# A constant row of a graph network: from a product on TensorE to an addition on VectorE

## The chip, the cores and the metric

One core of a Trainium2 chip runs the whole program in one launch. It has five engines with a queue of instructions each: PE (matrix products into PSUM), DVE (elementwise work, scans), ACT (activations and copies), POOL (here: indirect gathers) and SP (here: plain transfers). ACT issues transfers too. Engines wait for one another by semaphores. The metric is the device time of the program in microseconds (us).

## The reference

Two layers of a graph network on 100000 nodes and 50000 edges. In the first, rows of 32 edge values are summed, averaged and maximised over the edges of each source node, and a small network of two layers turns the 97 values of a node into 64:

```
h = concatenate([seg_sum, seg_max, seg_mean, u[batch]], axis=1)
h = relu(h @ W1 + b1)
x = x + (h @ W2 + b2)
h = jnp.maximum(_layernorm(x), 0.0)
agg = segment_sum(h[src], dst)
x = x + relu(agg @ W.T + b)
```

A node without edges still gets relu(u W1 + b1) @ W2 + b2, a constant row. The kernel adds that row to every node, and to the nodes with edges only the difference to it; so "layer two minus the constant" has to be formed for each of them.

## The kernel before

The edges are sorted by node on the chip (up to about 190 us of the profile). Then a **first pass** works through them in 98 steps (BLOCKS) of 512 edges, in 4 tiles (BT) of 128 rows; a **second pass** does the same for the second layer with other instructions, which the change doesn't touch. The order of each engine's queue is written out by hand: the engines run loops of their own over n, and in step n an engine takes different blocks for different jobs.

Step n of the first pass, engine by engine:

- POOL: four gathers of edge values for block n (L576), with waits for DVE's scans, dense additions and one-hots of earlier blocks.
- DVE: the two scans of block n (L1127, L1129), from PSUM p_g and the rows c_rows into feats; the dense addition of block n-7 (L1159); the scaling of gathered values of block n+2 (L1115); the one-hots of block n-5 (L1140).
- PE: the transposes of block n+1 (L1378) into p_g; the expansion of block n-6 (L1408 and L1403, one-hots times records, into p_t or p_u); layer two of block n-1 (function layer2); layer one of block n (L1383, from feats into p_z). An f32 product shows as two MATMUL records.
- ACT: the activation of block n-1 (L719, from p_z into hid); in every second step three loads of rows (L715); the record of block n-1 (L725 and L726) and its store (L731); two of the eight windows of block n-3 (L709, after registers with their starts are loaded, L701).
- SP: six windows of block n-3 (L406), and the dense rows in and out.

Layer two writes one PSUM tile, p_m[0], of 4 x 64 columns. It begins with one bf16 product of three ones rows with nc3, the negated constant split into three bf16 parts (L1389), which fills all 256 columns; the four products with W2 (L1391) add to it. They wait for the activation (hid_ok) and for the previous block's sums to be copied (copied). A record is 66 values for each edge: the 64 sums, the node's number as a key, and a pad. ACT writes it: `record` copies the key, then the sums, and `store_rec` sends it to memory; a ring of four holds the records. nc3 is made once, during the sort, by constant_c and three_parts on DVE beside a turn of the sort.

Of the kernel before, what the change touches and what calls it, by code (L numbers as in the profile page):

```python
# [9 lines left out]
BF16 = mybir.dt.bfloat16  # L10
F16 = mybir.dt.float16
ALU = mybir.AluOpType
# [56 lines left out]
def valid(n):  # L69

    return 0 <= n < BLOCKS


def build(nc, x, src, dst, edge_attr, u, W1, b1, W2, b2, W, b, out):
# [5 lines left out]
    with ExitStack() as ctx:  # L80
        def sb(name, shape, dt=F32):
            return ctx.enter_context(nc.sbuf_tensor(name, shape, dt))
# [4 lines left out]
        def sem(name):  # L87
            return ctx.enter_context(nc.semaphore(name))
# [6 lines left out]

        ident = sb("ident", [P, P])
        one = sb("one", [P, P])
        one_b = sb("one_b", [P, P], BF16)
        pos_i = sb("pos_i", [P, COLS], I32)
        pos_f = sb("pos_f", [P, COLS])  # L100
        next_pos = sb("next_pos", [P, COLS])
# [28 lines left out]
        r0 = sb("r0", [P, P])  # L130
        c_neg = sb("c_neg", [P, D])
        added_rows = sb("added_rows", [P, D])
        nc3 = sb("nc3", [P, BT, D], BF16)
        part_b = [sb(f"part_b{q}", [P, D], BF16) for q in range(2)]
        part_f = [sb(f"part_f{q}", [P, D]) for q in range(3)]
        c_bc = sb("c_bc", [P, D])
        relub = sb("relub", [P, D])

# [125 lines left out]
        rows_in = two("rows_in")  # L264
        scaled, turned, scanned, feats_ok = sem("scaled"), sem("turned"), sem("scanned"), sem("feats_ok")
        z_ok, hid_ok, m_ok = sem("z_ok"), sem("hid_ok"), sem("m_ok")
        copied = sem("records_copied")
        rec_out = several("rec_out", RRING)
        win_in = several("win_in", WRING)
        hot_ok, expanded, added = sem("hot_ok"), sem("expanded"), sem("added")  # L270
# [36 lines left out]
        def delta(k):  # L307
            side, n = divmod(k, BLOCKS)
            return p_d[side][n % len(p_d[side])][:, 0:BT * D].rearrange("p (t d) -> p t d", d=D)
# [201 lines left out]
        def _(pool):  # L511
# [3 lines left out]
            def link(ins):  # L515
                step[0] += 1
                ins.then_inc(s_pool, 1)
                pool.wait_ge(s_pool, step[0])
# [18 lines left out]
            link(g.tensor_scalar(span_f[:, :], prow_i[:, 0:SPAN], 0.5, None, ALU.add))  # L537
            link(g.memset(eps_t[:, :], EPS))
            link(g.memset(one[:, :], 1.0))
            link(g.memset(one_b[:, :], 1.0))  # L540
            link(g.memset(wrong[:, :], 0.0))
            link(g.memset(pad_rec[:, :], -1.0))
            link(g.memset(gagg[D:D + 1, :], 1.0))
# [101 lines left out]
        def _(act):  # L645
# [76 lines left out]
            def record(side, n):  # L722
                k = BLOCKS * side + n
                act.wait_ge(m_ok, k + 1)
                s.copy(rec[k % RRING][:, :, KEY], rn[side][:, BT * n:BT * (n + 1)])  # L725
                s.copy(rec[k % RRING][:, :, 0:D], delta(k)).then_inc(copied, 1)  # L726

            def store_rec(side, n):
                k = BLOCKS * side + n
                act.wait_ge(copied, k + 1)  # L730
                s.dma_start(rec_rows(side, n), rec[k % RRING][:, :, :].rearrange("p t r -> p (t r)")).then_inc(rec_out[k % RRING], 16)  # L731

# [63 lines left out]
        def _(dve):  # L796
# [44 lines left out]
                link(v.tensor_scalar(dummy_f[:, :], srcs_i[:, :], float(BLOCKS * STEP), None, ALU.add))  # L841
                link(v.tensor_scalar(next_pos[:, :], pos_f[:, :], 1.0, None, ALU.add))

            def three_parts(row, at):

                link(v.tensor_copy(part_b[0][:, :], row[:, :]))
                link(v.tensor_tensor(part_f[0][:, :], row[:, :], part_b[0][:, :], ALU.subtract))
                link(v.tensor_copy(part_b[1][:, :], part_f[0][:, :]))
                link(v.tensor_tensor(part_f[1][:, :], part_f[0][:, :], part_b[1][:, :], ALU.subtract))
                link(v.tensor_scalar(part_f[1][:, :], part_f[1][:, :], ident[:, at + 2:at + 3], None, ALU.mult))  # L850
                link(v.scalar_tensor_tensor(part_f[2][:, :], part_b[1][:, :], ident[:, at + 1:at + 2], part_f[1][:, :], ALU.mult, ALU.add))
                link(v.scalar_tensor_tensor(part_f[1][:, :], part_b[0][:, :], ident[:, at + 0:at + 1], part_f[2][:, :], ALU.mult, ALU.add))

            def constant_c():

                three_parts(c_neg, 0)
                link(v.tensor_copy(nc3[:, :, :], part_f[1][:, :].unsqueeze(1).to_broadcast([P, BT, D])))

            def constant_rows():

                link(v.tensor_scalar(part_f[1][:, :], c_bc[:, :], ident[:, CONST[0]:CONST[0] + 1], None, ALU.mult))
                link(v.scalar_tensor_tensor(added_rows[:, :], b_bc[:, :], ident[:, CONST[1]:CONST[1] + 1], part_f[1][:, :], ALU.mult, ALU.add))
                v.tensor_copy(rowmax[:, :], eps_t[:, :]).then_inc(s_wts, 1)

            def bounds(first_node_i):
# [36 lines left out]
            def beside_turn(t):  # L902

                if t == 0:
                    dve.wait_ge(s_const, 1)
                    dve.wait_ge(s_dstl, 96)
                    bounds(dn_i[:, 0:1])
                elif t == 1:
                    dve.wait_ge(s_dcast, 1)
                    link(v.tensor_tensor(ends[:, 1:COLS], dn_f[:, 1:COLS], dn_f[:, 0:COLS - 1], ALU.is_lt))  # L910
                elif t == 3:
                    link(v.reduce_sum(wrong[:, 2:3], ends[:, 1:COLS], AX.X))
                elif t == 6:
                    full = E // COLS
                    v.tensor_tensor(wrong[0:full, 3:4], pair[0:full, 1:2], pair[0:full, 0:1], ALU.is_lt)
                elif t == 4:
                    halves_first()
                elif t == 5:
                    row_of_empty()
                elif t == 7:  # L920
                    weights_turned()
                elif t == 8:
                    constant_c()
                elif t == 9:
                    constant_rows()
                elif t == 11:
                    positions()
# [216 lines left out]
            def add_dense(side, m):  # L1144
# [16 lines left out]
                    ins = v.scalar_tensor_tensor(dout[pair_ % ORING][:, b_, :], to[:, :], 0.0, din[pair_ % 2][:, b_, :], ALU.max, ALU.add)  # L1161
                ins.then_inc(added, 1)

            dve.wait_ge(s_cast, 2)
            dve.wait_ge(s_near, 1)
            dve.wait_ge(s_col, 1)
# [2 lines left out]
            for n in range(BLOCKS + SRC_ADD):  # L1169
                if valid(n):  # L1170
                    scans(n)
                if valid(n - SRC_ADD):
                    add_dense(0, n - SRC_ADD)
                if valid(n + 2):
                    scale_attr(n + 2)
                if valid(n - SRC_HOT):
                    onehots(0, n - SRC_HOT)
                if n == 0:
                    dst_group_starts()
                if n == 1:  # L1180
                    rows_above()
                if n == 3:
                    group_starts()
                    v.reduce_sum(wrong1[:, :], wrong[:, :], AX.X).then_inc(s_wrong, 1)
                if n == 5:
                    dve.wait_ge(s_wsum, 1)
                    v.tensor_scalar(fast[:, :], p_u[0:1, COLS - 1:COLS], 0.0, None, ALU.is_equal).then_inc(s_fast, 1)
# [113 lines left out]
        def _(pe):  # L1301
# [83 lines left out]
            def layer2(n):  # L1385
                pe.wait_ge(hid_ok, n + 1)
                if n >= 1:
                    pe.wait_ge(copied, n)
                mm(p_m[0][:, 0:BT * D], one_b[0:3, :], nc3[0:3, :, :].rearrange("p q d -> p (q d)"), start=True, stop=False)  # L1389
                for t in range(BT):  # L1390
                    last = mm(p_m[0][:, D * t:D * (t + 1)], hid[n % 2][:, P * t:P * (t + 1)], w2_s[:, :], start=False, stop=t == BT - 1)  # L1391
                last.then_inc(m_ok, 1)

            def expand(side, m):
# [99 lines left out]
```

## Time and profile before

| | us |
|---|---|
| median of 3 runs | 1320.73 |
| lowest and highest run | 1318.56, 1332.19 |
| span of the profiled execution, first to last instruction | 1509.9 |
| PE busy in it | 1105.5 |
| DVE busy | 1002.8 |
| POOL busy | 852.9 |
| ACT busy | 310.7 |

The profiled execution took longer than the runs that are timed without a profile; its span is all that is known of its own time. The sort fills the span up to about 190 us, the first pass runs to about 850 us, the second to the end. A row of a timeline gives the start, the duration, the engine, the line, and the tiles (out<-in); in brackets stand the idle time of the engine ahead of it and what ended it ("issue": nothing that the profile shows; "remote": a queue or core that it doesn't know). Rows of the kind ACTq and SPq are transfers being issued by that engine. PEld rows are weight loads, which run beside PE's products.

### The profile page before, as it was taken

The numbers are of one execution on the slowest core, as the hardware profiler recorded it, in microseconds if no ns is written. First come the engines' busy times: TensorE is split into PE (matmuls) and PEld (weight loads), VectorE is DVE, ScalarE is ACT, GpSimd is POOL, SyncE is SP. The second block draws the span as 40 slices with busy tenths as digits, with TensorE's granted clock in tenths as the row PEclk, the third lists the DMA queues.
The fourth block names the chain that finished last, engine by engine and source line by source line (L and its number), as shares of the span: only waits on it lengthen the run. The fifth ranks groups of instructions, "written<-read, shape, count | busy, mean of one in ns | idle before, by whom it ended". The sixth has DMA issues, their size and how long they took to land.

```text
span 1509.9 us, 20704 instructions
## 1 busy us (share of the span) xinstructions
PE 1105.5 (73%) x5924; PEld 841.3 (56%) x5924; DVE 1002.8 (66%) x2441; ACT 310.7 (21%) x781; POOL 852.9 (56%) x824
## 2 busy tenths in 40 slices
PE   0131177998988989998988515888787778787788
PEld 0010045666666666766766314766566656675667
DVE  9888986776777667767776324656656656565575
ACT  0630322222222222222222001111111111111110
POOL 3000266676666666767672266766667666676650
PEclk9985567998999888889898755868779787777879
DMA  1000035776776676767776824777777777777777
GB/s 42 0 0 1 25 72 121 185 197 174 184 184 185 170 180 173 183 166 197 172 186 160 202 53 105 170 161 170 157 169 167 158 160 158 172 172 156 164 158 164
DMA packets 492904, 217.97 MB, mean 144 GB/s; under 512 B 424120, under 2 KB 455836, under 8 KB 492786
## 3 DMA queue, kind: packets, MB, share of 16 engines
q1 hardware_dynamic: 357442, 134.88, 37.5%
q10 hardware_dynamic: 110256, 62.42, 15.9%
q0 software_dynamic: 25088, 19.32, 7.0%
q8 instruction: 48, 0.79, 0.2%
q14 instruction: 70, 0.57, 0.1%
HBM read 136.97 MB, written 79.45 MB: 143 GB/s over the span
## 4 chain that ended last, share of the span: by engine, by line
PE 57%; issue 13%; DVE 13%; ACTq 6%; another core or an unknown queue 5%; ACT 4%; DMA 0%; POOL 0%; SPq 0%; DVEq 0%; POOLq 0%
PE p_t L1403 8%; PE p_u L1403 7%; PE p_m L1391 7%; PE p_t L1408 6%; PE p_u L1408 5%; PE p_z L1383 5%; PE p_z L1403 4%; PE p_z L1408 3%; ACTq L709 3%; ACT hid L719 2%; PE p_g L1378 2%; PE p_g L1432 2%; DVE kb L974 2%; ACTq L701 2%
## 5 line engine op out<-in xcount | busy, mean ns | idle before, releaser
L576 POOL DMA_INDIRECT xa<-in_edge_attr_dram,gi x392 | 430.0, 1097 | 310.2 <-issue 115.2
L595 POOL DMA_INDIRECT xa<-node_table,gi x392 | 407.8, 1040 | 250.8 <-issue 117.5
L1140 DVE SCALAR_TENSOR_TENSOR shared<-win,node_of 112x1024 f32<-112x1024 f32 x98 | 118.9, 1213 | 207.6 <-remote 157.9
L1127 DVE TENSOR_TENSOR_SCAN feats<-c_rows,feats,p_g 64x512 f32<-64x512 f32 x97 | 123.2, 1270 | 105.3 <-remote 46.6
L719 ACT ACTIVATE hid<-p_z,bias_z 128x512 f32<-128x512 f32 x98 | 111.8, 1140 | 208.3 <-issue 178.1
L1408 PE MATMUL p_u<-one 128*128 128x512 f32 x230 | 127.8, 641 | 4.0 <-issue 4.0
L1140 DVE SCALAR_TENSOR_TENSOR oneh<-win,node_of 112x1024 f32<-112x1024 f32 x98 | 119.6, 1221 | 16.2 <-DMA win<-records 13.4
L1383 PE MATMUL p_z<-feats,w_s 96*128 96x512 f32 x196 | 127.5, 737 | 2.5 <-DVE feats L1129 2.5
L1408 PE MATMUL p_t<-one 128*128 128x256 f32 (+1 forms) x228 | 128.9, 654 | 0.3 <-issue 0.2
L1129 DVE TENSOR_TENSOR_SCAN feats<-c_rows,feats,p_g 32x512 f32<-32x512 f32 x97 | 123.3, 1271 | 1.4
L1391 PE MATMUL p_m<-w_s,hid 128*128 128x64 f32 x784 | 118.8, 299 | 0.0
L1432 PE MATMUL p_g<-ident,hn 128*128 128x128 f32 x196 | 50.3, 345 | 90.1 <-issue 53.3
L1403 PEld LDWEIGHTS p_t<-win,oneh 128*128 128x128 f32 x784 | 99.3, 198 | 30.1 <-issue 29.4
L1403 PEld LDWEIGHTS p_u<-win,oneh 128*128 128x128 f32 x784 | 97.6, 195 | 30.0 <-issue 26.8
L1391 PEld LDWEIGHTS p_m<-w_s,hid 128*128 128x128 f32 x784 | 104.6, 208 | 12.7 <-issue 2.0
L1211 DVE TENSOR_SCALAR hn<-xa,mv,rstd 128x64 f32<-128x64 f32 x392 | 99.1, 340 | 7.9 <-DVE rstd L1208 2.0
L1403 PEld LDWEIGHTS p_u<-win,shared 128*128 128x128 f32 x528 | 80.8, 228 | 41.2 <-issue 41.1
L767 ACT ACTIVATE sd<-mv,eps_t 128x4 f32<-128x4 f32 x98 | 29.2, 298 | 360.4 <-issue 274.8
L1403 PEld LDWEIGHTS p_t<-win,shared 128*128 128x128 f32 x528 | 79.1, 222 | 39.6 <-issue 39.5
L1403 PEld LDWEIGHTS p_z<-win,shared 128*128 128x128 f32 x512 | 73.5, 213 | 43.6 <-issue 43.0
L725 ACT COPY rec<-rn 128x4 f32<-128x4 f32 x196 | 37.7, 192 | 281.6 <-PE p_m L1391 162.0
L1403 PE MATMUL p_u<-win,oneh 128*128 128x64 f32 x784 | 94.6, 274 | 1.3 <-DVE oneh L1140 1.1
(270 smaller groups left out, 1609.7 us busy)
## 6 DMA issues: line engine op xcount, KB each, us to landing
win<-records SPq DMA_DIRECT2D x980, 28.9 KB
records<-rec ACTq DMA_DIRECT2D x196, 132.0 KB
node_table<-dout SPq DMA_DIRECT2D x49, 512.0 KB
din<-in_x_dram SPq DMA_DIRECT2D x48, 512.0 KB
din<-node_table SPq DMA_DIRECT2D x43, 512.0 KB
out_dram<-dout SPq DMA_DIRECT2D x43, 512.0 KB
c_rows<-rows_src ACTq DMA_DIRECT2D x141, 128.0 KB
win<-records ACTq DMA_DIRECT2D x588, 28.9 KB
```

The costliest lines, as they stand in the source:

```text
L576: g.indirect_dma_start(out=xa[n % XRING][:, t, 0:FE], out_offset=None, in_=edge_attr, in_offset=bass.IndirectOffsetOnAxis(ap=gi[0][:, BT * ...
L595: g.indirect_dma_start(out=xa[k % XRING][:, t, :], out_offset=None, in_=T, in_offset=bass.IndirectOffsetOnAxis(ap=gi[1][:, BT * n + t:BT * ...
L719: s.activation(hid[n % 2][:, :].rearrange("p (t n) -> p n t", n=P), p_z[n % 2][:, :].rearrange("p (n t) -> p n t", t=BT), ACT.Relu, bias=b ...
L1127: v.tensor_tensor_scan(f[0:64, :], c[0:64, at:at + BLK], p_g[n % 2][0:64, :], first[0:64], ALU.mult, ALU.add)
L1129: v.tensor_tensor_scan(f[64:96, :], c[64:96, at:at + BLK], p_g[n % 2][0:32, :], first[64:96], ALU.min, ALU.max).then_inc(feats_ok, 1)
L1140: v.scalar_tensor_tensor(hots[side][m % HRING][0:WP, :, :], win[k % WRING][0:WP, :, KEY:KEY + 1].to_broadcast([WP, PER, UNIT]), -float(STE ...
L1211: last = v.tensor_scalar(hn[n % 2][:, t, :], xa[(BLOCKS + n) % XRING][:, t, :], mv[n % 2][:, t, 0:1], rstd[n % 2][:, t:t + 1], ALU.subtrac ...
L1383: mm(p_z[n % 2][:, :], w1_s[:, :], feats[n % 2][:, :], start=True, stop=True).then_inc(z_ok, 1)
L1391: last = mm(p_m[0][:, D * t:D * (t + 1)], hid[n % 2][:, P * t:P * (t + 1)], w2_s[:, :], start=False, stop=t == BT - 1)
L1403: last = mm(to[:, D * s:D * (s + 1)], hots[side][m % HRING][:, s, :], win[k % WRING][:, s, 0:D], start=True, stop=True)
L1408: mm(bank[:, 0:width], one[:, :], one[:, :].unsqueeze(1).to_broadcast([P, width // P, P]), start=True, stop=True)
L1432: last = tr(p_g[n % 2][:, P * h:P * (h + 1)], hn[n % 2][:, 2 * h:2 * h + 2, :].rearrange("p t d -> p (t d)"), ident[:, :])
```

## The change

In the first pass, PE no longer multiplies the constant into the sums: the four products of layer two each start their own columns of p_m[0]. ACT copies only the key (a new semaphore, keys_copied, tells of it). DVE reads the sums from PSUM, adds the negated constant row c_neg and writes the 64 values of each record: `less_constant`, in DVE's step n for block n-1, behind the one-hots of block n-5. The store on ACT waits for both. The second pass keeps ACT's two copies. The three-part split, nc3 and the bf16 ones are gone; c_neg was there already.

```diff
-            link(g.memset(one_b[:, :], 1.0))
...
             def record(side, n):
                 k = BLOCKS * side + n
                 act.wait_ge(m_ok, k + 1)
-                s.copy(rec[k % RRING][:, :, KEY], rn[side][:, BT * n:BT * (n + 1)])
-                s.copy(rec[k % RRING][:, :, 0:D], delta(k)).then_inc(copied, 1)
+                keys = s.copy(rec[k % RRING][:, :, KEY], rn[side][:, BT * n:BT * (n + 1)])
+                if side == 0:
+                    keys.then_inc(keyed, 1)
+                else:
+                    s.copy(rec[k % RRING][:, :, 0:D], delta(k)).then_inc(copied, 1)
 
             def store_rec(side, n):
                 k = BLOCKS * side + n
+                if side == 0:
+                    act.wait_ge(keyed, k + 1)
                 act.wait_ge(copied, k + 1)
...
-            def three_parts(row, at):
...
-            def constant_c():
-
-                three_parts(c_neg, 0)
-                link(v.tensor_copy(nc3[:, :, :], part_f[1][:, :].unsqueeze(1).to_broadcast([P, BT, D])))
...
-                elif t == 8:
-                    constant_c()
...
+            def less_constant(n):
+
+                dve.wait_ge(m_ok, n + 1)
+                v.tensor_tensor(rec[n % RRING][:, :, 0:D], delta(n), c_neg[:, :].unsqueeze(1).to_broadcast([P, BT, D]), ALU.add).then_inc(copied, 1)
...
                 if valid(n - SRC_HOT):
                     onehots(0, n - SRC_HOT)
+                if valid(n - SRC_REC):
+                    less_constant(n - SRC_REC)
...
                 if n >= 1:
                     pe.wait_ge(copied, n)
-                mm(p_m[0][:, 0:BT * D], one_b[0:3, :], nc3[0:3, :, :].rearrange("p q d -> p (q d)"), start=True, stop=False)
                 for t in range(BT):
-                    last = mm(p_m[0][:, D * t:D * (t + 1)], hid[n % 2][:, P * t:P * (t + 1)], w2_s[:, :], start=False, stop=t == BT - 1)
+                    last = mm(p_m[0][:, D * t:D * (t + 1)], hid[n % 2][:, P * t:P * (t + 1)], w2_s[:, :], start=True, stop=True)
                 last.then_inc(m_ok, 1)
```

DVE's queue in the middle of the first pass, before: one-hots, then the scans of the next step.

```order
L1140 SCALAR_TENSOR_TENSOR oneh0<-win0,node_of 112x1024
L1127 SCALAR_TENSOR_TENSOR feats0<-c_rows1,feats1,p_g0 64x512
L1129 SCALAR_TENSOR_TENSOR feats0<-c_rows1,feats1,p_g0 32x512
L1159 TENSOR_TENSOR dout2<-p_u,din1 128x512
L1115 TENSOR_TENSOR xa4<-xa4,share 128x4x32
L1140 SCALAR_TENSOR_TENSOR oneh1<-win1,node_of 112x1024
```

The same stretch of DVE's queue in the changed kernel (lines are its own); rec is the record, p_m0 layer two's sums.

```order
L1124 SCALAR_TENSOR_TENSOR oneh0<-win0,node_of 112x1024
L1151 TENSOR_TENSOR rec0<-p_m0,c_neg 128x4x64
L1111 SCALAR_TENSOR_TENSOR feats0<-c_rows1,feats1,p_g0 64x512
L1113 SCALAR_TENSOR_TENSOR feats0<-c_rows1,feats1,p_g0 32x512
L1143 TENSOR_TENSOR dout2<-p_u,din1 128x512
L1099 TENSOR_TENSOR xa4<-xa4,share 128x4x32
L1124 SCALAR_TENSOR_TENSOR oneh1<-win1,node_of 112x1024
L1151 TENSOR_TENSOR rec1<-p_m0,c_neg 128x4x64
```

One addition stands between the one-hots of a step and the scans of the next; it waits for layer two (m_ok).

PE's queue at the same place, before.

```order
L1403 MATMUL p_t<-win0,oneh0 128x64 x8
L1389 MATMUL p_m0<-nc3,one_b 128x256
L1391 MATMUL p_m0<-w2_s,hid1 128x64 x4
L1383 MATMUL p_z0<-feats0,w1_s 128x512
L1378 MATMUL p_g0<-ident,xa0 64x128 x4
L1408 MATMUL p_u<-one 128x512
L1403 MATMUL p_u<-win1,oneh1 128x64 x8
```

PE's queue there in the changed kernel.

```order
L1393 MATMUL p_t<-win0,oneh0 128x64 x8
L1381 MATMUL p_m0<-w2_s,hid1 128x64 x4
L1374 MATMUL p_z0<-feats0,w1_s 128x512
L1369 MATMUL p_g0<-ident,xa0 64x128 x4
L1398 MATMUL p_u<-one 128x512
L1393 MATMUL p_u<-win1,oneh1 128x64 x8
```

The product of nc3 is gone, one in each of the 98 steps; nothing else moved.

## Rows read from the trace of the kernel before

**Rows 1.** Head of the page.

```profile
span 1509.9 us, 20704 instructions
```

**Rows 2.** Timeline of PE: eleventh and last step of the first pass.

```profile
274.45 0.28 PE L1389 MATMUL p_m<-nc,one_b 3*128 3x256 bf16 x1 [0.70 <-ACT hid L719]
...
834.28 0.28 PE L1389 MATMUL p_m<-nc,one_b 3*128 3x256 bf16 x1 [0.17 <-ACT hid L719]
```

**Rows 3.** Sums over stretches: stretch, length, busy by engine, clock, DMA share, GB/s.

```profile
274.00:834.00 560.00, 508.26 (x2863) 372.23 (x2863) 392.63 (x430) 140.03 (x262) 364.82 (x331) 0.90 0.70 180
...
1000.00:1200.00 200.00, 158.07 (x820) 127.41 (x819) 117.83 (x466) 31.08 (x127) 133.27 (x127) 0.80 0.74 162
```

**Rows 4.** Timeline of PE: a step of the first pass at full clock.

```profile
714.64 0.28 PE L1389 MATMUL p_m<-nc,one_b 3*128 3x256 bf16 x1
714.85 1.10 PE L1391 MATMUL p_m<-w_s,hid 128*128 128x64 f32 x8
...
719.83 0.28 PE L1389 MATMUL p_m<-nc,one_b 3*128 3x256 bf16 x1
```

**Rows 5.** Timeline of ACT in the same steps.

```profile
706.59 1.13 ACT L719 ACTIVATE hid<-p_z,bias_z 128x512 f32<-128x512 f32 x1 [2.77 <-issue]
...
711.48 1.14 ACT L719 ACTIVATE hid<-p_z,bias_z 128x512 f32<-128x512 f32 x1 [1.89 <-issue]
...
716.49 0.38 ACTq L731 DMA_DIRECT2D records<-rec  x1
...
722.14 0.20 ACT L725 COPY rec<-rn 128x4 f32<-128x4 f32 x1 [2.64 <-PE p_m L1391]
```

**Rows 6.** Groups of 274 to 834 us: busy us, mean ns, idle before.

```profile
L576 POOL DMA_INDIRECT xa<-in_edge_attr_dram,gi x329 | 362.8, 1103 | 164.4 <-issue 96.9 <-DVE feats L1129 37.2 <-DVE dout L1159 30.2
...
L1127 DVE TENSOR_TENSOR_SCAN feats<-c_rows,feats,p_g 64x512 f32<-64x512 f32 x86 | 109.3, 1271 | 96.2 <-remote 41.5 <-issue 27.5 <-PE p_g L1378 25.9
L1140 DVE SCALAR_TENSOR_TENSOR oneh<-win,node_of 112x1024 f32<-112x1024 f32 x87 | 106.2, 1221 | 11.3 <-DMA win<-records 8.6 <-issue 2.6
...
L726 ACT COPY rec<-p_m 128x256 f32<-128x256 f32 x87 | 31.9, 367 | 0.0
...
L1389 PE MATMUL p_m<-nc,one_b 3*128 3x256 bf16 x87 | 24.7, 284 | 51.9 <-ACT hid L719 29.7 <-issue 21.8
```

**Rows 7.** Timeline of DVE: one step without a wait inside.

```profile
600.83 1.27 DVE L1127 TENSOR_TENSOR_SCAN feats<-c_rows,feats,p_g 64x512 f32<-64x512 f32 x1
...
603.41 0.69 DVE L1159 TENSOR_TENSOR dout<-p_t,din 128x512 f32<-128x512 f32 x1
...
604.31 1.23 DVE L1140 SCALAR_TENSOR_TENSOR oneh<-win,node_of 112x1024 f32<-112x1024 f32 x1
```

**Rows 8.** Timeline of PE: layer two's start at the lower clock.

```profile
603.60 0.36 PE L1389 MATMUL p_m<-nc,one_b 3*128 3x256 bf16 x1 [1.09 <-ACT hid L719]
603.88 1.97 PE L1391 MATMUL p_m<-w_s,hid 128*128 128x64 f32 x8
```

**Rows 9.** Timeline of DVE in the sort: two sources, one in PSUM.

```profile
108.20 0.42 DVE L974 TENSOR_TENSOR kb<-p_t,kb 128x256 f32<-128x256 f32 x1
```

**Rows 10.** Timeline of POOL: a gather during a scan, one beside the one-hots.

```profile
602.03 0.94 POOL L576 DMA_INDIRECT xa<-in_edge_attr_dram,gi  x1 [0.30 <-issue]
...
604.53 1.83 POOL L576 DMA_INDIRECT xa<-in_edge_attr_dram,gi  x1 [0.30 <-issue]
```

**Rows 11.** Timeline of the sort: PE's turn and DVE's reader of it.

```profile
99.77 0.66 PE L1308 MATMUL p_t<-ident,ka 128*128 128x128 f32 x4 [2.07 <-DVE ka L975]
...
101.86 0.69 DVE L1013 TENSOR_TENSOR kb<-p_t,flip 128x512 f32<-128x512 f32 x1
```

**Rows 12.** Timeline of the first pass's start: ACT's key copy, DVE's group starts.

```profile
214.99 0.20 ACT L725 COPY rec<-rn 128x4 f32<-128x4 f32 x1 [8.52 <-PE p_m L1391]
...
217.76 0.98 DVE L895 SCALAR_TENSOR_TENSOR start_row<-start_f,limit 1x800 int32<-1x800 f32 x1 [4.29 <-issue]
```

More of the change, by code:

```diff
@@ L97, in build @@
         one = sb("one", [P, P])
-        one_b = sb("one_b", [P, P], BF16)
         pos_i = sb("pos_i", [P, COLS], I32)
@@ L132, in build @@
         added_rows = sb("added_rows", [P, D])
-        nc3 = sb("nc3", [P, BT, D], BF16)
-        part_b = [sb(f"part_b{q}", [P, D], BF16) for q in range(2)]
-        part_f = [sb(f"part_f{q}", [P, D]) for q in range(3)]
+        part_f = sb("part_f", [P, D])
         c_bc = sb("c_bc", [P, D])
@@ L266, in build @@
         z_ok, hid_ok, m_ok = sem("z_ok"), sem("hid_ok"), sem("m_ok")
-        copied = sem("records_copied")
+        copied, keyed = sem("records_copied"), sem("keys_copied")
         rec_out = several("rec_out", RRING)
@@ L842, in positions @@
                 link(v.tensor_scalar(next_pos[:, :], pos_f[:, :], 1.0, None, ALU.add))
-            def three_parts(row, at):
[L846 to L852, printed above, removed]
-            def constant_c():
-                three_parts(c_neg, 0)
-                link(v.tensor_copy(nc3[:, :, :], part_f[1][:, :].unsqueeze(1).to_broadcast([P, BT, D])))
             def constant_rows():
-                link(v.tensor_scalar(part_f[1][:, :], c_bc[:, :], ident[:, CONST[0]:CONST[0] + 1], None, ALU.mult))
-                link(v.scalar_tensor_tensor(added_rows[:, :], b_bc[:, :], ident[:, CONST[1]:CONST[1] + 1], part_f[1][:, :], ALU.mult, ALU.add))
+                link(v.tensor_scalar(part_f[:, :], c_bc[:, :], ident[:, CONST[0]:CONST[0] + 1], None, ALU.mult))
+                link(v.scalar_tensor_tensor(added_rows[:, :], b_bc[:, :], ident[:, CONST[1]:CONST[1] + 1], part_f[:, :], ALU.mult, ALU.add))
                 v.tensor_copy(rowmax[:, :], eps_t[:, :]).then_inc(s_wts, 1)
```

## The prediction

> **What bounds it now.** I read the page's head first, then the sums over stretches, the groups by line, and the timeline of single steps. The profiled span is 1509.9 us [rows 1]; the median of the runs is 1320.73 us, 0.875 of it, so the profile stretches the program. I make the sum in the profile's time and carry it over at the end.
>
> The change touches the first pass, 98 steps. The constant's product (L1389) starts at 274.45 us in its eleventh step and at 834.28 us in its last [rows 2]: 559.83 us for 87 steps, 6.43 us each. In that stretch PE is busy 508 of 560 us at a granted clock of 0.90, DVE 393 us, ACT 140 us, POOL 365 us [rows 3]. The clock was thus at the lower of its two levels (1.2 GHz) for about a fifth of the time. Three chains turn once in each step, and the timeline prices them.
>
> - PE alone: at the full clock the constant's product starts at 714.64 us and again at 719.83 us with no wait between [rows 4], a step of 5.19 us.
> - ACT and PE in turn: layer one's activation (L719) starts at 706.59 and the next one at 711.48 [rows 5], 4.89 us; between them lie its own time, the constant's product, layer two, ACT's two copies, the store's issue and the windows' issue. Often something in it is late. In every second step ACT also issues three loads of rows (L715); in one such step the key copy starts at 722.14 [rows 5], 1.0 us after layer two should have ended (719.83 + 0.21 + 1.10 = 721.14 by the two starts and the 1.10 us of [rows 4]). Of the 88 products from 274.45 on, 52 start within 0.08 us of the activation's end (the two of [rows 2] among them), and PE's idle time ahead of L1389 is 51.9 us [rows 6].
> - DVE: from the first scan at 600.83 to the end of the one-hots at 604.31 + 1.23 = 605.54 [rows 7], 4.71 us; then it waits for the transposes of the next step.
>
> So the step is PE's at the half clock and in the fastest steps, and the ACT–PE chain's elsewhere. L1389 is in both, behind its wait for the activation.
>
> **The product on PE.** 98 products go. From the start of one to the start of the first L1391 behind it is 0.21 us at the full clock (714.64 to 714.85) and 0.28 us at the half clock (603.60 to 603.88) [rows 4, 8]. I round the latter up to 0.30, since L1389's own time is 0.28 us in the one place and 0.36 in the other. A fifth of the steps at 0.30 and the rest at 0.21 give 98 × 0.228 = 22.3 us. It isn't hidden: the wait for the activation comes ahead of it.
>
> **The sums' copy moves from ACT to DVE.** The trace has no subtraction of a row from these sums on DVE. The nearest row is a two-operand DVE instruction of 256 columns with one source in PSUM, 0.42 us [rows 9]. From below I bound it by ACT's copy of the same tile, 0.37 [rows 6], from above by DVE's addition of 512 columns from PSUM, 0.69 [rows 7]. I take 0.42, the row of the same shape. Up to now the store is issued at 716.49, 0.54 us after layer two's end at 714.85 + 1.10 = 715.95 [rows 4, 5], with two copies on ACT between. Now the key copy on ACT and DVE's addition run side by side, so the store is issued as before if DVE is there in time, and the ACT–PE chain falls to 4.89 - 0.21 = 4.68 us.
>
> Is DVE there in time? The addition of step n-1 stands behind the one-hots of DVE's step n and ahead of the scans of step n+1. Behind it are queued those scans, the dense addition and the scaling; PE waits for them (layer one, transposes), and so does POOL. DVE's chain becomes 4.71 + 0.42 + 0.03 = 5.16 us a step, and it turns only when PE has finished layer two. What PE does next (layer one of n, transposes of n+2, the expansion) needs only what DVE finished ahead of that addition, so PE isn't held. Up to now DVE idled 96.2 us ahead of the scans in the 87 steps [rows 6]; those waits are for transposes and row loads that come earlier in the step than layer two's end, so the new wait takes their place and isn't added to them.
>
> DVE's 5.16 us is a new floor, though. Of the 87 steps 19 were shorter than 5.16 + 0.21 = 5.37 us, most of them the 5.19 of [rows 4]; each loses up to 0.18 of its gain, 3.5 us together, 4.0 over 98.
>
> **POOL.** A gather that starts beside the one-hots (SBUF sources only) takes 1.83 us, one that starts during a scan (a PSUM and an SBUF source) 0.94 [rows 7, 10]. The new addition is of the scan's kind, so I charge POOL nothing. Were it of the other kind, a gather could lose 0.9 us a step, and POOL's 4 × (1.103 + 0.30) = 5.61 us [rows 6, 10] would become 6.5, past today's 6.43. The Trainium skill, SBUF — State Buffer, section SBUF: two separate sides, says that a DVE instruction with two SBUF inputs locks the port pair that it shares with GpSimd. By that rule an addition with one PSUM input doesn't lock it and the sum stands; were it locked, some 7 us would come on top. The 1.83 and the 0.94 agree with the rule.
>
> **Setup and start.** The split of the constant into three parts goes, eight DVE instructions that stand ahead of the flip of a turn (L1013). PE's turn was ready at 99.77 + 0.66 = 100.43, and its reader started at 101.86 [rows 11]: -1.4 us. At the start of the pass DVE is now tied to PE: its scan of step 3 comes behind the addition of step 1, and that behind layer two, whose key copy started at 214.99 [rows 12]. Then follow the addition (0.42), two scans (2.55), the scaling (0.3) and the next addition (0.42), so the group starts move from 217.76 [rows 12] to about 218.7: +1.0 us.
>
> **Sum.** -22.3 + 4.0 - 1.4 + 1.0 = -18.7 us of 1509.9, 1.2%. Taken whole off the median it gives 1302 us, taken as a share 1304.4. In an unprofiled run the step is about 6.43 × 0.875 = 5.63 us (an estimate that spreads the stretch evenly), nearer to DVE's floor, so I take the smaller gain: **1304 us**. A measurement of this kernel tells about 1% (13 us) from no change.
>
> **Rivals.**
> - *Already on another floor* (0.30). At 5.63 us a step the unprofiled pass would stand next to POOL's 5.61, if gathers cost the same without a profile; then at most 98 × 0.02 = 2 us is to be had. Or its steps are mostly the 5.19 of PE at the full clock, and DVE's 5.16 leaves 98 × 0.03 = 3 us. For it: all chains lie close together. Against it: in the profile POOL waited 67 us for DVE (37.2 and 30.2) [rows 6], so it isn't the bound there. Time 1317 to 1321 us.
> - *DVE becomes the bound: slower* (0.13). One barrier now ties DVE, PE and ACT; where DVE is late, the store, the windows, the next activation and layer two are late too. If its waits on DMA stay (8.6 us for windows, and 41.5 us "remote" ahead of the scans, where row loads land [rows 6]: 0.58 us a step), its chain is 5.74 us. It decides from 5.63 us a step on; at 5.74 it costs 11 us, and with the 0.69 us bound of the addition 6.01, 37 us: 1332 to 1358 us, 1340 as its value. Against it: the later start of DVE's step should cover these waits.
> - *The clock* (0.03). With less work PE waits more, and a lower granted clock could take the gain back. A stretch of the second pass, where PE is busy 158 of 200 us, shows 0.80 against 0.90 here at 91% [rows 3]. At 0.80 a PE step of 4.98 us is 6.23, against 5.53 at 0.90: 98 × 0.7 = 69 us, less the gain, some 1370 us. The Trainium skill, TensorE: Matmul & The Clock Gate, part 1, says that the throttled state is the default and that activity releases it; by that rule the time would be 1370 us if PE's idle time grew as far as in the second pass, and the two stretches agree in direction. I give it little, since the work taken away is 4% of a step.
> - *More than the sum* (0.05). In the steps with row loads ACT comes late to the copies, and there it saves the sums' copy (0.37 in place of 0.21): 49 × 0.16 = 8 us more, 1288 to 1296 us.
> - That the product stays is no rival: no row of PE's order writes it any more.
>
> **Numbers.** My forecast (1296 to 1312 us) has 0.49, of which 0.41 below 1307.5 us. Faster by over 1%: 0.41 + 0.05 = 0.46. Slower by over 1%: 0.13 + 0.03 = 0.16. Within 1%: 0.38. The range for 8 in 10 goes from 1286 us (just past the most gain) to 1334 us (the other floors, and the mild end of a late DVE).
>
> **What would show it.** L1389's group is gone, and 98 additions of about 0.42 us stand on DVE, each behind layer two with a wait for PE; DVE's waits ahead of the scans shrink to little. Right: the step falls by about 0.2 us, most of layer two's first products start just behind an activation, and DVE takes no longer than 5.2 us from one addition to the next when nothing holds it. Wrong: ACT's store waits for DVE, gathers last longer beside the addition, the granted clock of the pass falls below 0.88, or the store is issued more than 0.6 us after layer two's end.

## The result and the profile after

The changed kernel takes 1318.62 us (median of 20 runs, 1309.34 to 1325.36) against 1327.99 us for the kernel before in the same comparison (20 runs, 1318.56 to 1335.88): a ratio of 0.9923 [0.9903, 0.9943]. It is faster by 0.8%, some 10 us. The forecast, 1304 us beside a median of 1320.73, stood for 16.7 us (18.7 us in its sum), and the prediction had set anything within 1% as no change. The time lies outside the forecast's 1296 to 1312 us, and inside its range of 1286 to 1334 us.

The profiled execution of the kernel before from which the prediction was read was itself stretched: 1509.9 us [rows 1], while a second profile of the same kernel spans 1321.4 us and fits the runs. Everything below compares with that second profile; it is one execution, as every profile here. The head of the page, first of the second profile of before, then of after:

```profile
core 0 of [0], span 1321.4 us
```

```profile
span 1314.3 us, 20596 instructions
```

Sums over the stretch from 260 to 700 us, which lies inside the first pass in both (stretch, length, busy of PE, weight loads, DVE, ACT and POOL, granted clock, DMA share, GB/s). Before, second profile:

```profile
260.00:700.00 440.00, 423.00 (x2649) 316.62 (x2649) 359.75 (x396) 130.11 (x242) 343.37 (x317) 1.00 0.83 213
```

After:

```profile
260.00:700.00 440.00, 418.00 (x2610) 320.85 (x2608) 397.18 (x491) 110.29 (x163) 340.58 (x326) 0.96 0.84 215
```

The work moved as the change says: ACT is busy 20 us less, DVE 37 us more, and POOL issues 326 gathers in the stretch instead of 317. The granted clock is 1.00 and 0.96, so the full level (2.4 GHz) holds nearly all the time in both, unlike the 0.90 of [rows 3].

Groups by line in that stretch (busy us, mean ns | idle us before, by releaser). Before, second profile:

```profile
L576 POOL DMA_INDIRECT xa<-in_edge_attr_dram,gi x317 | 343.5, 1084 | 96.7 <-issue 92.7 <-PE p_g L1378 2.4 <-DVE dout L1159 0.6
...
L1127 DVE TENSOR_TENSOR_SCAN feats<-c_rows,feats,p_g 64x512 f32<-64x512 f32 x79 | 100.0, 1265 | 1.9 <-issue 1.9
...
L1115 DVE TENSOR_TENSOR xa<-xa,share 128x128 f32<-128x128 f32 x79 | 23.1, 292 | 74.7 <-DMA xa<-in_edge_attr_dram,gi 71.6 <-issue 2.9
L1389 PE MATMUL p_m<-nc,one_b 3*128 3x256 bf16 x80 | 22.2, 278 | 1.7 <-ACT hid L719 1.6
```

After:

```profile
L572 POOL DMA_INDIRECT xa<-in_edge_attr_dram,gi x326 | 341.4, 1047 | 99.7 <-issue 85.8 <-DVE dout L1143 7.0 <-PE p_g L1369 4.6
...
L1151 DVE TENSOR_TENSOR rec<-p_m,c_neg 128x256 f32<-128x256 f32 x81 | 33.8, 418 | 19.0 <-PE p_m L1381 18.7
L1099 DVE TENSOR_TENSOR xa<-xa,share 128x128 f32<-128x128 f32 x82 | 23.6, 287 | 20.1 <-DMA xa<-in_edge_attr_dram,gi 19.6 <-issue 0.2
```

Here is what the stretched profile hid. In the normal execution POOL waits for almost nothing: 92.7 of its 96.7 idle us are "issue", 0.30 us ahead of each gather, and the 67 us of waits for DVE in [rows 6] are 1.5 us (by the waits of POOL), none longer than an issue. PE's idle time ahead of the product, 51.9 us in [rows 6], is 1.7 us. DVE, in turn, waits 71.6 us at the scaling for gathers to land. So the gathers stand back to back and set the pass, before and after. After the change the same number of them is done sooner because one takes 1047 ns in place of 1084, and DVE's waits for their landing fall from 71.6 to 19.6 us.

The ends of the two runs of gathers, in the timeline of POOL (start, us, engine, line; idle before in brackets), first of before (second profile), then of after:

```profile
174.68 1.16 POOL L576 DMA_INDIRECT xa<-in_edge_attr_dram,gi  x1 [114.08 <-ACT gi L734]
...
723.23 0.94 POOL L576 DMA_INDIRECT xa<-in_edge_attr_dram,gi  x1 [0.30 <-issue]
...
762.76 0.97 POOL L595 DMA_INDIRECT xa<-node_table,gi  x1 [32.12 <-SPq L438]
...
1281.21 0.94 POOL L595 DMA_INDIRECT xa<-node_table,gi  x1 [0.31 <-issue]
```

```profile
173.07 1.16 POOL L572 DMA_INDIRECT xa<-in_edge_attr_dram,gi  x1 [112.68 <-ACT gi L735]
...
710.45 0.94 POOL L572 DMA_INDIRECT xa<-in_edge_attr_dram,gi  x1 [0.31 <-issue]
...
756.29 0.97 POOL L591 DMA_INDIRECT xa<-node_table,gi  x1 [37.60 <-issue]
...
1274.98 0.95 POOL L591 DMA_INDIRECT xa<-node_table,gi  x1 [0.30 <-issue]
```

These rows split the difference of the two spans, 7.1 us, without a rest. The first gather starts 1.6 us sooner. The first pass's gathers take 538.3 us in place of 549.5, -11.2. From the last of them to the first of pass two it takes 44.9 us in place of 38.6, +6.3. Pass two takes 519.6 in place of 519.4, +0.2; the end 38.4 in place of 39.2, -0.8.

### The profile page after: what moved, and what is told of

Same layout as the page of the kernel before. It is cut to its first block and busy times, and to the rows that moved or that the text cites. A ratio compares the mean times of both kernels' runs of the same rounds, so it can differ in the third digit from the quotient of the medians.

```text
span 1314.3 us, 20596 instructions
## 1 busy us (share of the span) xinstructions
PE 990.4 (75%) x5826; PEld 778.5 (59%) x5826; DVE 1028.1 (78%) x2531; ACT 281.7 (21%) x683; POOL 825.9 (63%) x823
## 5 line engine op out<-in xcount | busy, mean ns | idle before, releaser
L572 POOL DMA_INDIRECT xa<-in_edge_attr_dram,gi x392 | 410.1, 1046 | 240.9 <-ACT gi L735 112.7
L591 POOL DMA_INDIRECT xa<-node_table,gi x392 | 400.4, 1021 | 156.9 <-issue 149.6
L1189 DVE BATCH_NORM_STATS2 stat<-xa 128x6 f32<-128x64 f32 x392 | 59.0, 213 | 168.3 <-DMA xa<-node_table,gi 168.2
L1381 PE MATMUL p_m<-w_s,hid 128*128 128x64 f32 x784 | 112.1, 289 | 29.5 <-ACT hid L715 29.0
L1398 PE MATMUL p_u<-one 128*128 128x512 f32 x230 | 119.9, 608 | 0.0
L1374 PE MATMUL p_z<-feats,w_s 96*128 96x512 f32 x196 | 115.7, 674 | 4.7 <-DVE feats L1113 4.7
L1398 PE MATMUL p_t<-one 128*128 128x256 f32 (+1 forms) x228 | 115.8, 594 | 0.0
L1393 PEld LDWEIGHTS p_t<-win,oneh 128*128 128x128 f32 x784 | 96.1, 193 | 24.6 <-issue 22.3
L1422 PEld LDWEIGHTS p_g<-ident,hn 128*128 128x128 f32 x196 | 25.6, 164 | 128.7 <-DVE hn L1202 128.3
L1393 PE MATMUL p_t<-win,oneh 128*128 128x64 f32 x784 | 93.5, 273 | 0.0
L1393 PEld LDWEIGHTS p_t<-win,shared 128*128 128x128 f32 x528 | 74.3, 217 | 20.1 <-issue 20.1
```

The source lines that it names most:

```text
L572: g.indirect_dma_start(out=xa[n % XRING][:, t, 0:FE], out_offset=None, in_=edge_attr, in_offset=bass.IndirectOffsetOnAxis(ap=gi[0][:, BT * ...
L591: g.indirect_dma_start(out=xa[k % XRING][:, t, :], out_offset=None, in_=T, in_offset=bass.IndirectOffsetOnAxis(ap=gi[1][:, BT * n + t:BT * ...
L1374: mm(p_z[n % 2][:, :], w1_s[:, :], feats[n % 2][:, :], start=True, stop=True).then_inc(z_ok, 1)
L1393: last = mm(to[:, D * s:D * (s + 1)], hots[side][m % HRING][:, s, :], win[k % WRING][:, s, 0:D], start=True, stop=True)
L1398: mm(bank[:, 0:width], one[:, :], one[:, :].unsqueeze(1).to_broadcast([P, width // P, P]), start=True, stop=True)
L1422: last = tr(p_g[n % 2][:, P * h:P * (h + 1)], hn[n % 2][:, 2 * h:2 * h + 2, :].rearrange("p t d -> p (t d)"), ident[:, :])
```

## Experiments

At first two theories were set against each other: the gathers set the pass (GATHER), or the chain of PE, ACT and DVE sets it (CHAIN). The last four runs take GATHER further: the sum's terms are right and the gathers hide them (COVERED); the change gains only because gathers meet less of the one-hots (PHASE); or it gains by the work that it moves (WORK). Ratios are to the kernel before, with 95% intervals, in two sets, each on one chip.

**A second profile of before.**

> The unchanged kernel, once more with a profile: the first profile of it took 1509.9 us where its runs take 1328, the changed kernel's profile 1314.3 us beside runs of 1319. If the stretch belonged to that one execution, the span is now 1315 to 1335 us. Theory GATHER (POOL's gathers set the first pass, in both kernels): from the eleventh step to the last the step is 5.40 to 5.55 us, and POOL stands idle only for its 0.30 us gaps. Theory CHAIN (PE and ACT set it before, POOL only after the change): the step is 5.55 to 5.75 us, and POOL waits for DVE 20 us or more in the pass.

The span was 1321.4 us, the execution's time 1323.19, and the step 5.49 us, as GATHER had it. The profile on which the prediction rests is no picture of a usual run.

**The product alone, taken out of before.**

```diff
-mm(p_m[0][:, 0:BT * D], one_b[0:3, :], nc3[0:3, ...], start=True, stop=False)
 for t in range(BT):
-    ... start=False, stop=t == BT - 1)
+    ... start=True, stop=True)
```

> The kernel before, with the constant's product left out and nothing in its place (ACT copies the sums as before; the first layer's rows carry the constant twice where a node has edges). It measures the product on PE by itself. CHAIN: 15 to 22 us faster than before (98 x 0.21 us), more than the change gave, since DVE has no addition. GATHER: 0 to 8 us faster, as much as the change gave or less.

Measured 0.9992 [0.9964, 1.0021], 1325.86 us. The 98 products are worth nothing that can be told from noise in the kernel before (at most 5 us by the interval). What PE no longer does it waits, for the scaling, which waits for gathers. Waits of PE from 260 to 700 us (times, longest), first of before (second profile), then without the product:

```profile
PE p_g L1378 <- DVE xa L1115: 15.0, 17, 2.2
```

```profile
PE p_g L1378 <- DVE xa L1115: 30.2, 24, 2.5
```

Its gathers (groups, 260 to 700 us) are those of before, to 7 ns:

```profile
L576 POOL DMA_INDIRECT xa<-in_edge_attr_dram,gi x316 | 344.8, 1091 | 96.3 <-issue 94.2 <-PE p_g L1378 1.8 <-DVE feats L1129 0.3
```

**The changed kernel with a product of zeros put back.**

```diff
+one_b = sb("one_b", [P, P], BF16)
+nc3 = sb("nc3", [P, BT, D], BF16)
+mm(p_m[0][:, 0:BT * D], one_b[0:3, :], nc3[0:3, ...], start=True, stop=False)
 ...
-    ... start=True, stop=True)
+    ... start=False, stop=t == BT - 1)
```

> The changed kernel, with a product of ones and zeros put back in front of layer two (a tile of zeros in place of the three-part constant; the result is the same). It measures what the addition on DVE costs while PE's work stays as it was. CHAIN: 15 to 22 us slower than the changed kernel, so 6 to 13 us slower than before. GATHER: 0 to 6 us slower than the changed kernel, so not slower than before.

Measured 0.9862 [0.9818, 0.9907], 1307.88 us. With PE's work back the kernel is not slower than the changed one but by its median faster (the two intervals meet at their ends). CHAIN had it slower by 15 to 22 us, GATHER by 0 to 6; that it could be faster neither had. Its gathers are shorter, 1006 ns, and DVE now waits for layer two ahead of the addition and hardly ever for landings:

```profile
L576 POOL DMA_INDIRECT xa<-in_edge_attr_dram,gi x333 | 335.0, 1006 | 106.3 <-issue 101.8 <-DVE feats L1117 3.9 <-PE p_g L1373 0.6
...
L1155 DVE TENSOR_TENSOR rec<-p_m,c_neg 128x256 f32<-128x256 f32 x83 | 35.3, 425 | 27.1 <-PE p_m L1386 27.1
```

**Only the wait.** Before, with nothing changed but that DVE waits for layer two, where the addition would stand.

```diff
 onehots(0, n - 5)
+dve.wait_ge(m_ok, n - SRC_REC + 1)
```

> The kernel before with only the wait of the change: DVE waits for layer two behind the one-hots, as in the changed kernel, but adds nothing; the product and ACT's copies stay. PHASE: the wait ties the one-hots to PE, the gathers' lost time changes by more than 5 us (49 us before) and the kernel's time follows it: 5 to 15 us faster if it falls as in the changed kernel. WORK: 0 to 8 us slower than before (only a wait is added).

Measured 0.9872 [0.9825, 0.9918], 1309.48 us: a wait and no other edit gives more than the whole change, by the ratios (0.9872 and 0.9923; the ends of the intervals overlap). The timeline shows how. Before, second profile, POOL and DVE together in one step:

```profile
410.19 0.94 POOL L576 DMA_INDIRECT xa<-in_edge_attr_dram,gi  x1 [0.30 <-issue]
...
411.12 1.22 DVE L1140 SCALAR_TENSOR_TENSOR oneh<-win,node_of 112x1024 f32<-112x1024 f32 x1
...
411.44 1.72 POOL L576 DMA_INDIRECT xa<-in_edge_attr_dram,gi  x1 [0.30 <-issue]
...
417.52 0.29 DVE L1115 TENSOR_TENSOR xa<-xa,share 128x128 f32<-128x128 f32 x1 [1.99 <-DMA xa<-in_edge_attr_dram,gi]
```

With the wait:

```profile
405.60 0.94 POOL L576 DMA_INDIRECT xa<-in_edge_attr_dram,gi  x1 [0.30 <-issue]
...
405.95 1.22 DVE L1140 SCALAR_TENSOR_TENSOR oneh<-win,node_of 112x1024 f32<-112x1024 f32 x1
...
406.86 1.13 POOL L576 DMA_INDIRECT xa<-in_edge_attr_dram,gi  x1 [0.31 <-issue]
...
407.75 1.27 DVE L1127 TENSOR_TENSOR_SCAN feats<-c_rows,feats,p_g 64x512 f32<-64x512 f32 x1 [0.58 <-PE p_m L1393]
```

A gather that starts while the one-hots run is longer, by nearly as much as what is left of them: started 0.32 us after their start it takes 1.72 us, 0.91 us after their start 1.13, otherwise 0.94. In both rows it ends 0.82 us behind their end. Before, DVE waits at the scaling for a gather to land and runs the one-hots right behind, so they mostly meet the next gather early. With the wait DVE goes by PE's beat, and the gathers start late in the one-hots.

**The other order on DVE.** Before, with the one-hots ahead of the scaling.

```diff
-if valid(n + 2):
-    scale_attr(n + 2)
 ... onehots(0, n - 5) ...
+if valid(n + 2):
+    scale_attr(n + 2)
```

> The kernel before with two DVE instructions exchanged: the one-hots ahead of the scaling, whose wait for a gather's landing set their start. No work is added or taken away. PHASE: the one-hots start about 3.2 us later in POOL's cycle of 1.25 us, so a gather starts some 0.75 us after them rather than 0.52; the gathers' lost time of the pass falls from 49 us to 20 to 35 us, and the kernel is 10 to 25 us faster than before. Theory WORK (the gain came from the work that the change moved or removed): 0 to 3 us either way.

Measured 0.9996 [0.9965, 1.0026], 1326.38 us, which is what WORK had said and PHASE had not. The gathers that met the one-hots did start later, 0.63 us after their start in the mean (0.47 before), and the loss is 47 us where 20 to 35 were expected. In the waits (engine, tile, line, releaser: us, times, longest) DVE still follows the landings:

```profile
DVE xa L1115 <- DMA xa<-in_edge_attr_dram,gi: 61.3, 44, 3.5
```

The timeline shows what took the later start back. The scaling has two SBUF sources too, and in 39 of the 85 meetings it now stands right behind the one-hots; 37 of these gathers end 0.82 us behind the scaling's end and not the one-hots':

```profile
407.69 1.22 DVE L1140 SCALAR_TENSOR_TENSOR oneh<-win,node_of 112x1024 f32<-112x1024 f32 x1
...
408.76 1.17 POOL L576 DMA_INDIRECT xa<-in_edge_attr_dram,gi  x1 [0.31 <-issue]
408.82 0.28 DVE L1115 TENSOR_TENSOR xa<-xa,share 128x128 f32<-128x128 f32 x1
```

So this run doesn't speak against the mechanism; its expectation had left the scaling out.

**The meeting taken away.** In the changed kernel the node numbers, the one-hots' second source, are put in a free PSUM bank, and the one-hots are issued as two instructions of 512 columns (the width of that tile).

```diff
-s.copy(node_of[:, :], node_of_i[:, :])
+s.copy(p_m[1][:, :], node_of_i[:, 0:COLS])
 ...
+for h in range(2):
+    v.scalar_tensor_tensor(hots[...][0:WP, 4*h:4*h+4, :], win[...][0:WP, 4*h:4*h+4, KEY:KEY+1]...,
+                           -float(STEP*m + COLS*h), p_m[1][0:WP, :]..., ALU.add, ALU.is_equal)
```

> The changed kernel, with the numbers that the one-hots are compared with in a PSUM bank (512 of them, two instructions of 512 columns in place of one of 1024), in both passes, so that no gather starts beside an instruction with two SBUF sources. GATHER: the gathers that took 1.2 to 1.9 us take 0.94, POOL's step falls from 5.41 to about 5.0 us, DVE's chain grows to about 5.3 us, and the kernel is 10 to 35 us faster than the changed one, the second pass included. CHAIN: POOL frees time that nobody uses, DVE's longer chain costs 0 to 15 us.

Measured **0.9483 [0.9445, 0.9522], 1254.5 us**, the fastest of all. DVE spends more (2 × 681 ns for what took 1.22 us), but nearly every gather takes its short time:

```profile
L572 POOL DMA_INDIRECT xa<-in_edge_attr_dram,gi x333 | 314.9, 946 | 103.5 <-issue 101.7 <-DVE feats L1114 1.5 <-PE p_g L1372 0.3
...
L1126 DVE SCALAR_TENSOR_TENSOR oneh<-win,p_m 112x512 f32<-112x512 f32 x176 | 112.5, 681 | 0.6 <-DMA win<-records 0.6
```

GATHER had expected 10 to 35 us over the changed kernel; it is 64 by the medians and 58 by the ratios. The edit serves both passes: in the profiles the first pass's gathers take 504.7 us in place of 538.3, the second's 489.5 in place of 519.6. The edit also splits the one-hots in two, and no run splits them without moving the source; but the 80 gathers that start in such a half with over 0.15 us of it left take 0.94 us, while those that start early in the scaling (0.29 us, two SBUF sources) do get longer, so the sources decide and not the length. A gather beside the scaling in the kernel before with the same edit:

```profile
428.80 0.28 DVE L1116 TENSOR_TENSOR xa<-xa,share 128x128 f32<-128x128 f32 x1
428.84 1.06 POOL L576 DMA_INDIRECT xa<-in_edge_attr_dram,gi  x1 [0.30 <-issue]
```

**The same in the kernel before, and in the kernel with the product of zeros.** The same edit of the one-hots.

> The kernel before, with the one-hots' numbers in PSUM as in nodes_psum, so that no gather is held up by them (POOL's step about 5.0 us). Theory COVERED (the sum's terms are right, and the gathers' floor hides them): PE's 5.19 us step or the ACT-PE chain is now over POOL's, so this is 10 to 20 us slower than nodes_psum (1254 us). Theory PHASE (the change's only gain is that gathers meet less of the one-hots): there is nothing left to gain, this is within 6 us of nodes_psum, and rather faster, since the changed kernel needs about 6 us longer from its last gather to the second pass.

> The kernel nodes_psum with the product of ones and zeros back in front of layer two: the product's price where gathers aren't held up. COVERED: 10 to 17 us slower than nodes_psum (98 x 0.17 us, PE's 5.19 against POOL's 5.02). PHASE, with PE still under the floor: 0 to 5 us slower.

Measured 0.9616 [0.9577, 0.9654], 1275.45 us, and 0.9618 [0.9577, 0.9659], 1273.91 us. Where the gathers aren't held up, the product has its price: with it the ratio is higher by 0.0133 and 0.0135, 18 us of 1327 (by the medians 21 and 19), give or take 7 by the intervals. That is COVERED's forecast, at its upper end, and not PHASE's. And now POOL waits for DVE. In the kernel with zeros DVE waits 18.2 us for layer two ahead of the addition; in the other one most of what DVE waits for ahead of the scans (32.8 us) is nothing that the profile names. Groups, 260 to 700 us, first of before with the edit, then of the kernel with zeros:

```profile
L576 POOL DMA_INDIRECT xa<-in_edge_attr_dram,gi x332 | 315.5, 950 | 123.7 <-issue 94.7 <-DVE feats L1130 19.8 <-DVE oneh L1142 7.8
```

```profile
L576 POOL DMA_INDIRECT xa<-in_edge_attr_dram,gi x335 | 316.2, 944 | 124.1 <-issue 87.9 <-DVE feats L1118 34.1 <-PE p_g L1376 1.8
```

**The kernels side by side**, over the last 352 of the first pass's 392 gathers, worked out from their timelines. "Lost" is the sum of the gathers' time above 0.944 us each; the step is that of layer two from the 11th to the 98th.

| kernel | ratio | step, us | gather start to start, us | lost, us |
|---|---|---|---|---|
| before (second profile) | 1 | 5.49 | 1.390 | 49 |
| before without the product | 0.9992 | 5.52 | 1.392 | 50 |
| one-hots ahead of the scaling | 0.9996 | 5.49 | 1.383 | 47 |
| after | 0.9923 | 5.43 | 1.357 | 36 |
| before with the wait alone | 0.9872 | 5.30 | 1.328 | 20 |
| after with a product of zeros | 0.9862 | 5.29 | 1.332 | 22 |
| before, node numbers in PSUM | 0.9616 | 5.31 | 1.319 | 2 |
| the same with addition and zeros | 0.9618 | 5.24 | 1.322 | 0 |
| after, node numbers in PSUM | 0.9483 | 5.02 | 1.260 | 1 |

In the upper six the step is, to 0.07 us, four times the gathers' distance, and within the intervals the ratio goes with the loss. In the two kernels that have the product and no losses the step is PE's 5.19 us [rows 4] and a little, 5.31 and 5.24. The wait alone and the product of zeros stand at 5.30 and 5.29 with some 20 us of losses, so in them PE's work sets the first pass as much as the gathers do (PE is busy 407 of 410 us from 260 to 670 us in each), and what the two kernels with the edit are faster by lies mostly in the second pass, 490 us of gathers there in place of 523. In the last one it is that of four undisturbed gathers, 4 × 1.25 = 5.0 us.

## Why the prediction failed

**The step that failed** is its reading of what bounds the pass: "the step is PE's at the half clock and in the fastest steps, and the ACT–PE chain's elsewhere", and the answer to its own rival *Already on another floor*, that POOL waited 67 us for DVE, "so it isn't the bound there". POOL's gathers were the bound, 0.30 us apart; taken off PE alone, the products only became waits of PE for what gathers bring. The row of the 67 us came from the stretched execution, whose span of 1509.9 us against a median of 1320.73 the text noted, and then spread evenly as a factor of 0.875. The stretch was not even: the first gather starts at 174.7 us in both profiles of before, so the sort had none of it, and in the normal execution the clock of the pass is full, PE's and DVE's chains are shorter, and POOL hardly waits. The prediction worked out that an unprofiled step of 5.63 us stood next to POOL's 5.61, gave this 0.30, and let a row from the other regime overrule it. That rival named the right mechanism. Its time, 1317 to 1321 us, is set against a median of 1320.73; the two medians in the comparison are 1327.99 and 1318.62, so the gain it allows, up to 3 us, was too small. It took POOL's floor for fixed, and the floor moved.

**Why the floor moved.** [Rows 10] held the key: a gather beside the one-hots took 1.83 us, one beside a scan 0.94. The prediction asked only whether the new addition would lengthen gathers. It did not ask when in the one-hots a gather starts. Of the 88 one-hots in the table's stretch (87 with the wait alone), before 79 have a gather that starts well inside them (over 0.03 us after their start and 0.02 us before their end), 0.47 us after their start in the mean. With the wait alone 85 have, but 0.86 us after it, with the product of zeros all 88, 0.84 us after, and more than half of the loss is gone. In the changed kernel 57 have, 0.47 us after, as early as before, and 31 escape. In most of these a gather has started just ahead of the one-hots, keeps its 0.95 us, and the next one starts as they end (POOL and DVE of after):

```profile
504.05 0.95 POOL L572 DMA_INDIRECT xa<-in_edge_attr_dram,gi  x1 [0.30 <-DVE dout L1143]
504.07 1.24 DVE L1124 SCALAR_TENSOR_TENSOR oneh<-win,node_of 112x1024 f32<-112x1024 f32 x1
...
505.30 0.95 POOL L572 DMA_INDIRECT xa<-in_edge_attr_dram,gi  x1 [0.30 <-DVE oneh L1124]
```

The Trainium skill, SBUF — State Buffer, section SBUF: two separate sides, says that a DVE instruction with two SBUF inputs locks a port pair that it shares with GpSimd, against a GpSimd instruction that reads SBUF (a gather reads its row numbers, gi, there). With one of the one-hots' sources in PSUM the mean gather was 946 ns, so these runs agree.

**Why the whole change gave less than its wait alone.** Without the product the engines' chain can go faster than four gathers (5.0 us), here 4.84 to 4.88 us a step. Layer two in the timeline of PE, after:

```profile
489.26 1.10 PE L1381 MATMUL p_m<-w_s,hid 128*128 128x64 f32 x8
...
494.14 1.06 PE L1381 MATMUL p_m<-w_s,hid 128*128 128x64 f32 x8
...
498.98 1.06 PE L1381 MATMUL p_m<-w_s,hid 128*128 128x64 f32 x8
```

So DVE catches up with the gathers again, waits for a landing (19.6 us above), and the one-hots fall on a gather's start. With the product PE's 5.19 us is slower than 5.0, POOL keeps just ahead, and the meeting stays late, where it costs less. A step of after, DVE and POOL together:

```profile
509.53 0.29 DVE L1099 TENSOR_TENSOR xa<-xa,share 128x128 f32<-128x128 f32 x1 [0.69 <-DMA xa<-in_edge_attr_dram,gi]
...
509.74 1.22 DVE L1124 SCALAR_TENSOR_TENSOR oneh<-win,node_of 112x1024 f32<-112x1024 f32 x1
...
510.30 1.48 POOL L572 DMA_INDIRECT xa<-in_edge_attr_dram,gi  x1 [0.30 <-issue]
```

That PE's beat keeps the meeting late is read from these traces and from the two runs that have both the wait and the product; no run varied the beat step by step.

**The terms.**
- *The product, -22.3 us*: of the right size, in a place that didn't count. Taken out of before it gave nothing to be told from noise; with undisturbed gathers the product alone was worth 18 us, beside the 22.3, and the whole change 18 us as well, beside the sum's 18.7 (each give or take 7).
- *The addition*: 418 ns against 0.42, and free: the kernel with zeros, which has it, stands at 0.9862, the one with the wait alone at 0.9872. Gathers were not lengthened by it: with the addition and the edit in PSUM they stay at 944 ns.
- *DVE's floor of 5.16 us, +4.0*: wrong. Where DVE doesn't wait, one addition follows another after 4.88 us, since DVE's instructions overlap a little, as in the timeline of DVE (after), where the scan starts 0.34 us behind an addition of 0.41:

```profile
500.35 0.41 DVE L1151 TENSOR_TENSOR rec<-p_m,c_neg 128x256 f32<-128x256 f32 x1
...
505.23 0.41 DVE L1151 TENSOR_TENSOR rec<-p_m,c_neg 128x256 f32<-128x256 f32 x1
505.57 1.26 DVE L1111 TENSOR_TENSOR_SCAN feats<-c_rows,feats,p_g 64x512 f32<-64x512 f32 x1
```

- *Setup, -1.4*: the first gather starts 1.6 us sooner. *Start, +1.0*: the group starts moved from 218.24 to 217.14, so against that gain about +0.5.
- *Missed*: +6.3 us between the passes. Layer two's last product ended 18.8 us after the last gather before, and 24.4 us after it in the changed kernel (by the timelines), so 5.6 of it lie there. These are single executions: without the product, where the gathers end no sooner than before, the stretch was 42.6 us in place of 38.6, so a part of it may be chance.

**The signs.** The step fell by 0.06 us and not 0.2. DVE's additions stood under 5.2 us apart where nothing held them. The waits ahead of the scans are gone (groups of after, whole run), but they were 1.9 us in the second profile of before already, so this sign tells nothing of the change:

```profile
L1113 DVE TENSOR_TENSOR_SCAN feats<-c_rows,feats,p_g 32x512 f32<-32x512 f32 x97 | 123.3, 1271 | 1.4
L1111 DVE TENSOR_TENSOR_SCAN feats<-c_rows,feats,p_g 64x512 f32<-64x512 f32 x97 | 122.4, 1262 | 0.0
```

From the eleventh step on the store was issued 0.55 to 3.48 us after layer two's end, 0.61 in the median (0.53 before), past the 0.6 named as a sign of failure in 45 of 88 steps. No run shows that this cost anything; POOL, which sets the pass, doesn't wait for it. The granted clock was 0.96, not below 0.88, so that rival is out; nor did DVE become the bound.

**Open.** What stretched the one profiled execution of before wasn't found. There DVE waits 41.5 us ahead of the scans for what the trace calls "remote" [rows 6], and ACT 58.1 us ahead of the key copies; in the same part of the second profile of that kernel there is no such wait.

## What to carry to other kernels

Before a sum is made on a profile, its span is to stand beside the median of the runs; where they differ by more than the runs do, take the profile again, and trust no wait in it that a second one doesn't show. Where an engine's instructions stand back to back with no wait for another engine (here 0.30 us of issue ahead of each gather), it is the bound, and what its work costs beside another engine's is to be asked first: here moving one operand of the one-hots to PSUM gave 3.8% in the kernel before, and taking 98 products off PE nothing until then. Two engines that disturb one another at some phase can gain or lose a per cent by a wait alone, so an edit's effect is to be told apart from the wait that it brings.

## What the runs showed of the hardware

A gather that starts during a DVE instruction with two SBUF sources ends 0.82 us behind that instruction's end: in the kernels whose one-hots read SBUF alone and stand behind the scaling, 465 gathers that started inside the one-hots, over 0.06 us from their start and 0.14 from their end, ended 0.81 to 0.83 us behind them. So 1.72 us with 0.90 us left, 1.13 with 0.31 left, and 0.94 beside scans or beside one-hots with a source in PSUM. The scaling, 0.29 us with two SBUF sources, does the same: 0.04 us into it a gather takes 1.06 us in place of 0.94. It costs little because few gathers start there (0.5 us over 352 gathers in the last kernel of the table). The 112 x 512 one-hots with a source in PSUM took 681 ns, two of them 12% longer than the one of 1024 columns from SBUF (1.22 us). The gathers of 128 rows stood at best 1.25 us apart, 0.94 us and 0.30 of issue.
